# Expert results written into the output's rows: gather, sum on VectorE, plain scatter

## The reference, cut to what matters

```python
# x: (6250, 256); 8 experts, the best 2 of each row are used
probs = softmax(xt @ Wr + br); top_p, top_idx = top_k(probs, 2)
weights = top_p / top_p.sum(-1)
xn = layernorm(xt)
xe = xn * ln_g[e] + ln_b[e]
y = gelu(xe @ W1[e] + b1[e]) @ W2[e] + b2[e]
out = (weights * y_of_the_two_experts).sum(axis=1)
x = x + out
```

## Time and profile before

| | us |
|---|---|
| median of 3 runs | 3451.92 |
| lowest, highest | 3440.41, 3462.80 |
| the profiled execution, its own time | 3448.99 |
| its span in the trace | 3447.4 |
| PE busy in the span | 2345.9 (68%) |
| POOL busy in the span | 1915.7 (56%) |
| DVE busy in the span | 1535.9 (45%) |

### The profile page before, as it was taken

How to read it: one execution, slowest core, us unless ns; L and a number is a source line. 1 busy time by engine, 2 the same in 40 slices (tenths; PEclk the granted TensorE clock), 3 DMA queues, 4 the chain that set the end, 5 groups by cost and what they waited for, 6 DMA issues and landing times. The chain is left out here.

```text
span 3447.4 us, 47206 instructions
## 1 busy us (share of the span) xinstructions
PE 2345.9 (68%) x11708; PEld 1576.6 (46%) x11709; DVE 1535.9 (45%) x4138; ACT 830.1 (24%) x1644; POOL 1915.7 (56%) x2043
## 2 busy tenths in 40 slices
PE   1478888888876666353666665454443379999996
PEld 1245555555542443131333332221211179999996
DVE  7444444555444334113455544322312056666663
ACT  2233333333231121021111000000000035555543
POOL 0364445455665666635666666666666545655553
PEclk6588989889897777566677666665565589999998
DMA  5232222222232233213333333333333443333334
GB/s 165 87 86 62 63 61 74 68 78 82 84 89 86 84 90 88 80 51 102 97 100 93 93 100 92 89 95 90 91 96 93 119 121 71 73 72 73 72 48 105
DMA packets 163077, 298.23 MB, mean 87 GB/s; under 512 B 47543, under 2 KB 106656, under 8 KB 162752
## 3 DMA queue, kind: packets, MB, share of 16 engines
q0 software_dynamic: 96736, 235.19, 26.2%
q1 hardware_dynamic: 41476, 39.54, 3.7%
q10 hardware_dynamic: 24732, 22.06, 2.1%
HBM read 255.78 MB, written 47.27 MB: 88 GB/s over the span
## 5 line engine op out<-in xcount | busy, mean ns | idle before, releaser
L755 POOL DMA_INDIRECT rows<-table,srcT x1568 | 1544.6, 985 | 1026.2 <-issue 505.1
L821 PE MATMUL bank<-rows,onehot 128*128 x1952 | 670.5, 484 | 685.0 <-POOLq L743 409.0
L821 PEld LDWEIGHTS bank<-rows,onehot 128*128 x1952 | 217.4, 111 | 1101.1 <-issue 975.3
L781 DVE SCALAR_TENSOR_TENSOR onehot<-iota_row,tbase,dstT 128x512 f16 x488 | 366.5, 753 | 685.5 <-issue 439.8
L1895 ACT ACTIVATE hid<-bank,b 128x256 f32<-128x256 f32 x432 | 179.1, 465 | 290.8 <-PE bank L1847 270.4
L1845 PE MATMUL bank<-W_high,hid_high 128*128 128x256 f32 x864 | 244.8, 283 | 0.0
L1845 PE MATMUL bank<-xe_high,W_high 128*128 128x256 f32 x864 | 241.2, 279 | 4.9 <-DVE xe_low L1928 4.9
L1847 PE MATMUL bank<-xe_high,W_low 128*128 128x256 f32 x864 | 240.1, 278 | 0.0
L1846 PE MATMUL bank<-xe_low,W_high 128*128 128x256 f32 x864 | 240.1, 278 | 0.0
L1846 PE MATMUL bank<-W_low,hid_high 128*128 128x256 f32 x864 | 239.8, 278 | 0.0
L1847 PE MATMUL bank<-W_high,hid_low 128*128 128x256 f32 x864 | 239.8, 278 | 0.0
(11 more groups left out here) (348 smaller groups left out, 3803.5 us busy)
## 6 DMA issues: line engine op xcount, KB each, us to landing
rows<-table,srcT POOLq DMA_INDIRECT x1568
W<-in_L_ffn_W_dram SPq DMA_DIRECT2D x14, 1024.0 KB
x_res<-in_x_dram SPq DMA_DIRECT2D x1, 6144.0 KB, 22.6
normal<-xn ACTq DMA_DIRECT2D x11, 528.0 KB
table<-part ACTq DMA_DIRECT2D x11, 512.0 KB
totals<-x_res SPq DMA_DIRECT2D x11, 512.0 KB, 6.8
table<-part SPq DMA_DIRECT2D x6, 512.0 KB, 2.9
table<-part_b SPq DMA_DIRECT2D x6, 512.0 KB, 2.9
```

The source lines that it names most:

```text
L755: nc.gpsimd.indirect_dma_start(out=rows[:, k % (M * U), 0:ROW], out_offset=None, in_=q.table, in_offset=bass.IndirectOffsetOnAxis(srcT[:, ...
L781: last = nc.vector.scalar_tensor_tensor(onehot[:, ds(slot, U), :], iota_row[:, :].unsqueeze(1).to_broadcast([P, U, P]), base, dstT[:, ds(k ...
L821: last = nc.tensor.matmul(acc[:, 0:ROW], hots[:, ds(hot0 + s * P, P)], ring_rows[:, ds(row0 + s * ROW, ROW)], start=False, stop=False, ski ...
```

## The change

The tensor `totals` and the copy at the end are gone. Layer 1 writes x into `out` itself (the last group only its 106 real rows). In the expert stage GpSimd, after the load and the scatter of a tile, gathers the rows of `out` for the tile whose results come next into the new tile `base`; DVE adds share x `b2` to it and then result x share, and GpSimd scatters the sum over the same rows, without adding. Padded places have the row number 6272, which is past the end and left out by a bounds check, in gather and scatter. The rows of one expert are all different; two experts may share rows, so in the second tile of each expert GpSimd waits, between its scatter and its gather, until every scatter up to the expert before has landed. The row numbers are moved on by DVE now (`to_new` after the share, `to_old` after the stores of the tile before have landed). One iota at layer 1's start is gone.

```diff
-                sp.dma_start(totals[NPAD:NPAD + TT, :].rearrange("(s p) d -> p s d", p=P),
-                             zeros[:, :].unsqueeze(1).to_broadcast([P, SUB, D])).then_inc(X["totals_begun"], 16)
...
-                    sp.dma_start(totals[t * P:(t + w) * P, :].rearrange("(t p) d -> p t d", p=P),
-                                 x_cols(t, w).rearrange("p (t d) -> p t d", d=D)).then_inc(X["totals_begun"], 16)
+                    if t + w < NT:
+                        sp.dma_start(out[t * P:(t + w) * P, :].rearrange("(t p) d -> p t d", p=P),
+                                     x_cols(t, w).rearrange("p (t d) -> p t d", d=D)).then_inc(X["out_begun"], 16)
+                    else:
+                        sp.dma_start(out[t * P:N, :], x_cols(t, w)[0:N - t * P, :]).then_inc(X["out_begun"], 16)
...
-                nc.gpsimd.iota(to_list[:, :], pattern=[[0, LCOLS // SUB], [1, SUB]], base=NPAD,
-                               channel_multiplier=SUB).then_inc(R["spares_ready"], 1)
...
-                copied_out(sp, 0, GROUPS // 2 * W)
-                sp.wait_ge(X["copied_out"], 16 * (GROUPS + 1))
...
-                def shift_to(n, at):
-                    shift.begin(n)
-                    pool.wait_ge(X["y_ready"], n * SUB + 1)
-                    settled(pool)
-                    for newer, older in ((to_mid[:, :], to_old), (to_new[:, :], to_mid), (to_list[:, at], to_new)):
-                        shift.link(nc.gpsimd.tensor_copy(older[:, :], newer))
-                        settled(pool)
...
                         nc.gpsimd.indirect_dma_start(
-                            out=totals, out_offset=bass.IndirectOffsetOnAxis(to_old[:, s:s + 1], axis=0),
-                            in_=ys[:, s, :], in_offset=None, compute_op=ALU.add).then_inc(X["y_out"], 16)
+                            out=out, out_offset=bass.IndirectOffsetOnAxis(to_old[:, s:s + 1], axis=0),
+                            in_=ys[:, s, :], in_offset=None, bounds_check=N - 1, oob_is_err=False).then_inc(X["y_out"], 16)
+
+                def load_base(n):
+
+                    pool.wait_ge(X["rows_kept"], n + 1)
+                    settled(pool)
+                    for s in range(SUB):
+                        nc.gpsimd.indirect_dma_start(
+                            out=base[:, s, :], out_offset=None, in_=out,
+                            in_offset=bass.IndirectOffsetOnAxis(to_new[:, s:s + 1], axis=0),
+                            bounds_check=N - 1, oob_is_err=False).then_inc(X["base_loaded"], 16)
 
                 def tile(b, e, j, n, step):
                     at = ds(narrow(pool.snap(e * ECOLS + j * SUB), 0, LCOLS - SUB), SUB)
                     load(n, at)
-                    shift_to(n, at)
-                    pool.wait_ge(X["totals_begun"], 16 * (LAST + 2))
+                    pool.wait_ge(X["out_begun"], 16 * (LAST + 1))
                     settled(pool)
                     store(n)
+                    step()
+                    load_base(n)
+
+                nothing_yet = (lambda b, e, pair: None)
+
+                def expert_before_is_out(b, e, pair):
+                    n = pool.value_load(lists[0:1, ds(e + 2 * E1, 1)], min_val=0, max_val=E1 * (NPAD // TT + 1))
+                    pool.wait_ge(X["y_out"], n * (16 * SUB) + 2 * 16 * SUB)
+
+                expert_tiles(pool, tile, None, (nothing_yet, expert_before_is_out))
...
-                def results_out(n):
+                def results_out(n, b):
+                    dve.wait_ge(X["base_loaded"], n * (16 * SUB) + 16 * SUB)
+                    dve.wait_ge(X["rows_kept"], n + 1)
+                    for s in range(SUB):
+                        nc.vector.scalar_tensor_tensor(base[:, s, :], b2[b][:, :], share_of_tile[:, s:s + 1], base[:, s, :],
+                                                       ALU.mult, ALU.add).then_inc(X["base_summed"], 1)
+                    dve.wait_ge(X["y_out"], n * (16 * SUB) + 16 * SUB)
+                    nc.vector.tensor_copy(to_old[:, :], to_new[:, :])
                     dve.wait_ge(X["y_ps"], n + 1)
-                    dve.wait_ge(X["y_out"], n * (16 * SUB) + 16 * SUB)
-                    dve.wait_ge(X["b2_known"], n * KNOWN + KNOWN)
+                    dve.wait_ge(X["base_summed"], n * SUB + SUB)
...
                 def tile(b, e, j, n, step):
+                    at = ds(narrow(dve.snap(e * ECOLS + j * SUB), 0, LCOLS - SUB), SUB)
                     dve.wait_ge(X["xs_turned"], CREDIT + n + 1)
...
-                    for s in range(SUB):
-                        nc.vector.tensor_scalar(b2_of_tile[:, s, :], b2[b][:, :], share[:, s:s + 1], None,
-                                                ALU.mult).then_inc(X["b2_known"], 1)
-                    nc.vector.tensor_copy(share_of_tile[:, :], share[:, :]).then_inc(X["b2_known"], 1)
+                    settled(dve)
+                    nc.vector.tensor_copy(share_of_tile[:, :], share[:, :])
+                    nc.vector.tensor_copy(to_new[:, :], to_list[:, at]).then_inc(X["rows_kept"], 1)
```

More of the change, by code:

```diff
@@ L1373, in program @@
         lng = [sb(f"lng_{b}", [P, 2 * C], F32, ffn) for b in range(2)]
-        names = ("raw_loaded small_loaded first_raw_loaded first_small_loaded high_ready weights_ready b2_known xs_loaded xs_turned share_taken rows_known xe_high "
-                 "xe_ready g1_ps gelu_done hid_high hid_ready y_ps y_ready y_out expert_done totals_begun all_out copied_out").split()
+        names = ("raw_loaded small_loaded first_raw_loaded first_small_loaded high_ready weights_ready xs_loaded xs_turned share_taken rows_known xe_high "
+                 "xe_ready g1_ps gelu_done hid_high hid_ready y_ps y_ready y_out expert_done out_begun base_loaded base_summed rows_kept").split()
         X = {n: sem("x_" + n) for n in names}
@@ L1659, in _ @@
                 dve.wait_ge(R["cols_ready"], 1)
-                dve.wait_ge(R["spares_ready"], 1)
                 nc.vector.tensor_copy(iota_cols[:, :], from_list[:, :])
-                nc.vector.tensor_copy(place_f[:, :], place[:, :]).then_inc(R["cols_ready"], 1)
-                start.link(nc.vector.tensor_copy(spare_to[:, :], to_list[:, :]))
+                start.link(nc.vector.tensor_copy(place_f[:, :], place[:, :]))
+                dve.sem_inc(R["cols_ready"], 1)
                 chain = Chain(dve, "layer1_chain", 64)
@@ L1694, in program @@
         ys = sb("ys", [P, SUB, D], F32, ffn)
-        rows_of, to_new, to_mid, to_old = (sb(name, [P, SUB], I32, ffn) for name in
-                                           ("rows_of", "to_new", "to_mid", "to_old"))
+        rows_of, to_new, to_old = (sb(name, [P, SUB], I32, ffn) for name in
+                                                ("rows_of", "to_new", "to_old"))
+        base = sb("base", [P, SUB, D], F32, ffn)
         xe = sb("xe", [P, C, TT], F32, ffn)
@@ L1700, in program @@
         hid_high, hid_low = (sb(f"hid_{n}", [P, HC, TT], FR, ffn) for n in ("high", "low"))
-        b2_of_tile = sb("b2_of_tile", [P, SUB, D], F32, ffn)
         share, share_of_tile = (sb(name, [P, SUB], F32, ffn) for name in ("share", "share_of_tile"))
         PAIRS = HC // 2
-        KNOWN = SUB + 1
-        def copied_out(eng, first, last):
-            eng.wait_ge(X["all_out"], 1)
-            for r0 in range(first, last, W):
-                r1 = min(r0 + W, last)
-                k = GW if r1 - r0 == W else 1
-                eng.dma_start(out[r0:r1, :].rearrange("(p k) d -> p (k d)", k=k),
-                              totals[r0:r1, :].rearrange("(p k) d -> p (k d)", k=k)).then_inc(X["copied_out"], 16)
         def expert_tiles(eng, body, before_expert=None, beside=(), after_expert=None):
```

35 lines of the change are left out of this document (14 added, 21 removed).

## The result

| | before | after |
|---|---|---|
| median, us | 3452.89 (20 runs) | 3468.37 (20 runs) |
| lowest, highest | 3440.41, 3469.47 | 3442.91, 3482.27 |
| the profiled execution, span | 3447.4 | 3465.7 |

The account below looks back on a forecast made before the run. TensorE bounds the expert tiles; 31 us at the end lack cover. 3447.4 - 25.2 + 1.4 - 1.1 + 0 = 3422.5 span, plus 1.6 = 3424.1; with the profile 2.9 under the median, forecast 3427, range 3408 to 3458.

Parts of the forecast that it names:

- Part 1: Kernel's end: copy out goes, two scatters and their landing remain, then 0.4 us to the span's end; gain 25 us.
- Part 2: GpSimd's steady tile: scatters and base gathers sum to 9.2 of 11.37 us, next load on time; cost 0.
- their landing is covered by 11 us: Steady tile: base rows are used one tile later, so their landing, at most 2.3 us, is hidden.
- Part 3: VectorE's steady tile: 1.2 us of work ahead of ys fits 1.56 us of idle time; cost 0.
- 1.4 us of register work: VectorE at experts' first tiles: new address work ahead of share, 0.2 us each, 7 times.
- Part 4: Landing wait once per expert on GpSimd: later gathers and loads still reach PE in time; no stall.
- 0.5 us to spare: Expert 1: second load landed by 2889.0, PE transposes at 2889.47.
- (a): Dearer scatter or bounds checks cause stalls of 1 to 3 us per expert: 3436 to 3448, chance 0.2.
- Part 5: Layer 1's start: one iota leaves GpSimd's way to the first gather; gain 1.1 us, between 0 and 1.1.
- (b): GpSimd bounds every tile through dear bounds-checked DMAs (d, price of one, at 2.0): about 3521, chance 0.13.
- (c): More gain than summed; no row has a mechanism beyond about 2 us, only the spread of runs; chance 0.05.

Follow-up runs that it names:

- e4: e1 without the gathers of base and VectorE's wait for their landing, base cleared once: 3428.75 us, against 3448.35 for the kernel before.
- e2: The kernel before, only addresses changed so that xe and hid lie where the changed kernel has them: 3468.17 us, ratio 1.0056 to before.
- e1: The changed kernel with xe, hid and their parts put back at their old addresses: 3449.5 us, ratio 1.0005 to the kernel before.
- e5: e1 with the scatter adding to the rows again instead of writing over them: 3472.35 us, against 3448.35 for the kernel before.
- e7: e1 with base gathered from the input x and no landing wait once per expert: 3469.17 us, against 3448.35 for the kernel before.
- e11: The kernel before plus two spare 64-byte-row gathers per tile, into a tile nobody reads: 3511.01 us, against 3457.26 for before.
- e14: The kernel before plus one spare 64-byte-row gather per tile, without bounds check: 3481.8 us, against 3462.53 for before.
- e15: e14 with a bounds check on its spare gather: 3478.36 us, against 3462.53 for the kernel before.
- e9: e1 with base gathers of 64 bytes a row instead of 1,024, from the input x: 3456.48 us, against 3446.21 for the kernel before.
- e8: The kernel before with its adding scatter going straight into out, bounds-checked, without totals and the copy: 3435.94 us, ratio 0.9969 to before.
- e12: The kernel before plus two spare plain DMAs of fixed 64-byte rows per tile: 3453.14 us, against 3457.26 for before.
- e6: The kernel before with a plain scatter that writes over the rows of totals instead of adding: 3430.68 us, against 3448.35 for before.

## Why the prediction was wrong, point by point

The profiled span is 43.2 us over the forecast of 3422.5. Of that 31.8 are the stretch (33.2 against 1.4), 8.5 the end, and 2.9 the start (1.8 later instead of 1.1 earlier, which is within what the gather stages vary).

- **Part 1, the end: right mechanism, a term missing.** Scatters at 1.02 and 1.01 (taken: 1.03 and 0.98). The gap was 0.9 (taken 0.5) and the landing 1.4 (taken 2.3), so that the sum to the landing, 5.1 against 5.6, held in part by luck. The failed step is "with 0.4 to the end of the span": it had to be GpSimd's DRAIN, 9.20 us. The row was in the trace of before, at 3424.6 for 7.32 us; I didn't ask what else the copy covered.
- **Part 2, GpSimd's steady tile: prices right, "cost 0" wrong.** This is the step that failed most. Scatter 1.02 and 1.00, base gather 1.05 and 1.02, issued from 2842.83 to 2847.85; the next load goes out in time. The new sum held up the second load by little: it took 1.11 us at 2839.80, beside the sum that began at 2839.18, against 0.98 in the earlier trace rows. But e4 shows that these gathers, with VectorE's wait for them, cost 21.5 us, as late starts of ACT, third tiles and a slower pace in some tiles. I had only asked whether GpSimd has room, not what its DMAs do to other engines. Wrong too is "their landing is covered by 11 us": by the part's own times the gathers end at 2855.2 and VectorE's sum with `base` begins near 2859.3, 4 us later. The trace of after has 4.0 us in the median, and where the landing took longer VectorE waited (10 times, 15.4 us, up to 3.8).
- **Part 3, VectorE: the work right, the wait ahead of it left out.** The sum with `base` took 0.87 and the index copy 0.16, in the idle time; e4 keeps all of that at 628.3. The wait for the landing of `base` is in no term. The 1.4 us of register work can't be told apart.
- **Part 4, the landing wait: the wait right, the slack too thin to be a forecast.** It came 8 times with 2.1 us each, and PE waited for `xs` in no tile but the first. The "0.5 us to spare" was real as a danger: third tiles lost 5.0 us in after (2.7 of them the pace, by e2) and 6.1 in e1. And rival (a)'s mechanism is what e5, e7, e11, e14 and e15 show, at 6 to 9 us a hit; I had priced it at 1 to 3, from the landing of a store, where a landing of `xs` as late as 7.2 us stops PE, and the clock falls behind the stop.
- **Part 5, the iota:** below what a profile tells.
- **Not in the prediction: the places of tiles.** No part asked what the new tile does to the addresses of the others. The sum puts them at nothing without a word. They cost 15.1 us by e2 and 10.1 by e1, a third to a half of the stretch's loss, and turned a kernel level with before (e1, 1.0005) into a slower one.
- **Rivals.** (a)'s time, 3436 to 3448, was too low, though for part of the reason given; (b) didn't happen (d = 1.0); e11 with its six DMAs, two of them adding, comes nearest to it, with PE waiting for `xs` 49.9 us in 20; (c) no.

## What to carry to other kernels

When work at the end of a kernel goes away, list everything that ran under it, block-end drains too, before booking the gain. A change that adds, drops or reorders on-chip tiles moves all later ones: compare the distance of products in both traces first, and give the moved tiles their old addresses before judging the rest. And where a helper engine has only a microsecond or two before another engine's long instruction and a large load, as GpSimd had here (1.7), one more DMA a tile can cost 6 to 9 us at each such place: what was accumulated by the store is better left there than gathered, summed and stored.

## What the runs showed of the hardware

- The same fp32r products stand 0.113 us apart or 0.117 to 0.121 when nothing but tile addresses is changed (e2), at the same granted clock of 1.00 (its level of 2.4 GHz). Whole tiles can also run at 0.118 beside others at 0.113 at the same addresses (e1, e9).
- GpSimd's DRAIN at the end of a block with indirect DMAs took 4.6 us behind the gather stages, 7.3 in before, e2 and e8, 7.9 in e5, e11 and e12, 3.9 in e14 and e15, and 9.0 to 9.2 in after, e4, e6 and the others with plain scatters. What it waits for wasn't tried.
- A plain scatter of 128 rows of 1 KB occupies GpSimd for 1.02 us, the adding one for 1.6; a bounds check adds nothing that can be seen (adding scatter 1.55 in e8, 1.54 in the earlier trace rows).
- Gathers issued beside the loads of the next expert let PE start only 6.5 us (e14) and 7.2 us (e7) after the second was out, and 2.3 us (e15, expert 6) where no 2 MB load runs; the last stores of the kernel landed within 2.3 us.
- Behind each such stop of PE (4.4 to 5.9 us in e7, e11, e14 and e15) the granted clock fell from 1.00 to 0.50, its level of 1.2 GHz (e7: 2908 to 2912).
